# Last mixture of a decoder kernel: sorted rows that carry residual, weight and token; masks made by GpSimd

## The reference, cut to what matters

```
h = x + _attention(_rmsnorm(x, g1), wq, wk, wv, wo)
return h + _moe(_rmsnorm(h, g2), router_w, router_b, w1, w2, w3)

def _moe(x, router_w, router_b, w1, w2, w3):
    xf = x.reshape(n, d)                               # n = 2048
    vals, idx = jax.lax.top_k(xf @ router_w + router_b, 2)
    scores = jax.nn.softmax(vals, axis=-1)
    cap = int(np.floor(n * CAP_FRAC))                  # 256
    oh = jax.nn.one_hot(idx, E, dtype=jnp.float32)     # 8 experts
    pos = jnp.cumsum(jnp.cumsum(oh, axis=0), axis=1).astype(jnp.int32)
    emask = oh * (pos < cap)
    tmask = jnp.sum(emask, axis=-1)
    assign = jnp.einsum('tke,e->tk', emask, jnp.arange(E, dtype=jnp.float32)).astype(jnp.int32)
    m = jnp.max(assign, axis=-1)                       # one expert per token
    y = y_all[m, jnp.arange(n)]       # gelu((xf @ w2[m]) * (xf @ w1[m])) @ w3[m]
    slot = jnp.where(tmask[..., None] > 0, y[:, None, :], xf[:, None, :])
    return jnp.einsum('tkD,tk->tD', slot, scores)
```

## Time and profile before

| | us |
|---|---|
| median of 3 runs | 1674.38 |
| lowest, highest | 1672.79, 1678.52 |
| the profiled execution, its time | 1675.38 |
| its span, first to last instruction | 1673.6 |
| busy: PE, DVE, ACT, POOL | 1423.6, 966.6, 749.0, 232.3 |

### The profile page before, as it was taken

One profiled execution on the slowest core, in us unless ns is written; L12 is line 12 of the kernel. 1 busy time (PEld: TensorE's weight loads), 2 busy tenths in 40 slices (PEclk: granted clock), 3 DMA queues, 4 the chain that ended last, 5 costly groups with the idle time before them and its releaser, 6 DMA issues.

```text
span 1673.6 us, 43831 instructions
## 1 busy us (share of the span) xinstructions
PE 1423.6 (85%) x17681; PEld 878.2 (52%) x17681; DVE 966.6 (58%) x2541; ACT 749.0 (45%) x1927; POOL 232.3 (14%) x201
## 2 busy tenths in 40 slices
PE   4889888696499999999958999889989898999672
PEld 3343434393266666766633466346644564456462
DVE  4354635323477777777723676576665776477532
ACT  1323142251266666666613276327723672447431
POOL 1011120123030030200010200030002100120124
PEclk7989999797799999999978899999989998899897
DMA  9600000023230100100021000000000000000012
GB/s 327 264 17 1 17 1 7 17 58 98 77 140 4 26 19 10 35 4 16 4 76 43 1 2 2 5 7 2 2 5 7 2 2 1 7 1 1 6 55 70
DMA packets 62072, 60.07 MB, mean 36 GB/s; under 512 B 27952, under 2 KB 47024, under 8 KB 60720
## 3 DMA queue, kind: packets, MB, share of 16 engines
q1 hardware_dynamic: 59536, 53.04, 10.0%
q0 software_dynamic: 2048, 4.20, 0.9%
q10 hardware_dynamic: 288, 0.03, 0.0%
HBM read 32.73 MB, written 24.51 MB: 34 GB/s over the span
## 4 chain that ended last, share of the span: by engine, by line
PE 69%; DVE 15%; issue 4%; SPq 4%; DMA 3%; ACT 3%; POOL 2%; ACTq 0%; POOLq 0%; DVEq 0%
PE ps L1126 7%; PE ps L1514 6%; PE ps L1533 5%; PE ps L500 5%; PE ps L1547 4%; PE ps L1106 4%; PE ps L1116 4%; DVE arena L586 4%; PE ps L1147 4%; PE ps L258 4%; PE ps L1502 3%; PE ps L474 3%; PE ps L1161 2%; PE ps L1556 2%; PE ps L797 2%
## 5 line engine op out<-in xcount | busy, mean ns | idle before, releaser
L1259 DVE TENSOR_REDUCE nmax<-ps 128x1 f32<-128x512 f32 x256 | 166.8, 683 | 56.3 <-PE ps L1116 55.7
L1590 ACT ACTIVATE arena<-ps,arena 128x512 f32<-128x512 f32 (+3 forms) x256 | 135.5, 531 | 119.1 <-DVE arena L1650 112.9
L1650 DVE TENSOR_REDUCE arena<-ps 128x1 f32<-128x512 f32 (+3 forms) x256 | 124.3, 487 | 78.8 <-PE ps L1518 76.7
L1219 ACT ACTIVATE arena<-ps,nmax 128x512 f32<-128x512 f32 x172 | 119.0, 692 | 80.8 <-DVE nmax L1259 79.3
L1533 PE MATMUL ps<-sqc,arena 128*128 128x128 f32 x640 | 106.6, 287 | 20.0 <-DVE arena L1658 19.7
L586 DVE TENSOR_REDUCE arena<-ps 128x8 f32<-128x1232 f32 x64 | 89.2, 1438 | 40.3 <-PE ps L462 40.1
L258 PE MATMUL ps<-identb 128*128 128x512 bf16 x408 | 110.0, 430 | 1.4 <-DVE kcol L707 1.4
L1267 DVE COPY arena<-ps 128x512 f32<-128x512 f32 x128 | 88.0, 688 | 39.9 <-PE ps L1126 38.4
L1514 PE MATMUL ps<-arena 64*128 64x384 f32 (+3 forms) x512 | 106.2, 493 | 0.0
L1658 DVE TENSOR_SCALAR arena<-arena 128x512 f32<-128x512 f32 (+3 forms) x256 | 100.8, 394 | 9.1
L598 DVE RECIPROCAL arena<-ps 128x128 f32<-128x128 f32 x8 | 7.7, 959 | 160.4 <-PE ps L500 160.4
(11 more groups left out here) (350 smaller groups left out, 2713.1 us busy)
## 6 DMA issues: line engine op xcount, KB each, us to landing
xs_d<-onehot SPq DMA_DIRECT2D x3, 3072.0 KB, 29.6
cw<-in_cw SPq DMA_DIRECT2D x2, 2048.0 KB, 13.4
rv<-in_rv SPq DMA_DIRECT2D x2, 1536.0 KB, 19.7
late<-in_gw SPq DMA_DIRECT2D x3, 1024.0 KB, 10.8
arena<-xs_d SPq DMA_DIRECT2D x46, 64.0 KB, 1.8
xs_d<-arena SPq DMA_DIRECT2D x46, 64.0 KB, 1.6
xs_d<-onehot SPq DMA_DIRECT2D x1, 2560.0 KB, 22.4
onehot<-q_s SPq DMA_DIRECT2D x96, 8.0 KB
```

The lines of the kernel that those rows point to most:

```text
L1219: nc.scalar.activation(PB[k % 6], ps[:, k % 5, :], ACT.Exp, bias=nmax[:, u:u + 1], accum_out=rsum[:, b % 2, u:u + 1]).then_inc(SD["exp"], 1)
L1259: nc.vector.tensor_reduce(nmax[:, k % NU:k % NU + 1], ps[:, k % 5, :], AX.X, ALU.max, negate=True)\
L1590: nc.scalar.activation(TF["p%d" % (n % 2)][:, h * S:h * S + wd], ps[:, FSB[n % 2][h], 0:wd], ACT.Exp, bias=TF["nmax"][:, k4:k4 + 1], accum ...
L1650: nc.vector.tensor_reduce(TF["nmax"][:, k4:k4 + 1], ps[:, FSB[n % 2][h], 0:wd], AX.X, ALU.max, negate=True)\
```

## The change

**Rows of G.** The sorted rows become 258 floats wide (`GW4`): normed row, residual, kept weight, and a token number. They live in `G4`, which takes the place of `cw1` and `cw2` (now one tensor `cw`), and go to a new HBM buffer `gs_d` of 23,552 rows. The token number is stored less 4096, so that a row that was never sent, all zero, gives number 4096 after the correction, beyond the output's 2048 rows, and is dropped by the bounds check. DVE's last operation of a tile does weight * y + residual, and POOL scatters the tile straight to the output. The gathers, the adds, the write-back and the output stores go.

**Who does what.** The weight copies of G move from POOL to ACT, behind each `linear` and ahead of the gelu. POOL instead makes an index and issues one indirect DMA per tile. SP only loads. `gs_d` is zeroed by `pool_G_zero`, four DMAs from the POOL queue between `pool_C` and `pool_D`.

**Masks.** `dve_prepare` keeps only pcol and moves to `dve_X` ahead of `dve_masks`; the rest is `pool_prepare`, ahead of `selw` on POOL, with a semaphore `s_mask` for which DVE (before L410) and PE wait.

```diff
-            else:
-                dve_prepare(dve)
...
+            if b == 0:
+                dve.wait_ge(s_mask, 1)
...
             if k == "B" and b == 0:
+                dve_prepare(dve)
                 dve_masks(dve)
...
-            pe.wait_ge(s_prep, 4)
+            pe.wait_ge(s_mask, 1)
...
+        def pool_prepare(pool):
+
+            pool.wait_ge(s_const[1], 16 * len(GROUPS[1]))
+            nc.gpsimd.tensor_copy(xmask[:, :, 0:KP], xmask_in)
+            nc.gpsimd.tensor_copy(xmask[:, :, KP:KW], xmask_in[:, :, 0:KW - KP])
+            for mask, given in ((amask, amask_in), (kmask, kmask_in)):
+                nc.gpsimd.memset(mask[:, :, KS:KP], MASKED)
+                nc.gpsimd.tensor_scalar(mask[:, :, 0:KS], given[:, :, :], MASKED, None, ALU.mult)
+                ins = nc.gpsimd.tensor_scalar(mask[:, :, KP:KW], given[:, :, 0:KW - KP], MASKED, None, ALU.mult)
+            ins.then_inc(s_mask, 1)
+            nc.gpsimd.tensor_copy(cpick[:, :, :], causal_in[:, 0:2, :])
+            nc.gpsimd.tensor_copy(cmask[:, :, :], causal_in[:, 2:4, :]).then_inc(s_mask, 1)
+
         def dve_prepare(dve):
 
             dve.wait_ge(s_const[1], 16 * len(GROUPS[1]))
-            nc.vector.tensor_copy(xmask[:, :, 0:KP], xmask_in)
-            nc.vector.tensor_copy(xmask[:, :, KP:KW], xmask_in[:, :, 0:KW - KP])
-            for mask, given in ((amask, amask_in), (kmask, kmask_in)):
-                nc.vector.memset(mask[:, :, KS:KP], MASKED)
-                nc.vector.tensor_scalar(mask[:, :, 0:KS], given[:, :, :], MASKED, None, ALU.mult)
-                ins = nc.vector.tensor_scalar(mask[:, :, KP:KW], given[:, :, 0:KW - KP], MASKED, None, ALU.mult)
-            ins.then_inc(s_prep, 1)
-            nc.vector.tensor_copy(cpick[:, :, :], causal_in[:, 0:2, :])
-            nc.vector.tensor_copy(cmask[:, :, :], causal_in[:, 2:4, :])
             nc.vector.tensor_reduce(pcol[:, :], vmask[:, :, :], AX.X, ALU.max).then_inc(s_prep, 1)
-            dve.wait_ge(s_prep, 5)
+            dve.wait_ge(s_prep, 4)
...
+        GW4 = 2 * P + 2
+        G4 = cw[:, 0:NTT * GW4].rearrange("p (t n) -> p t n", n=GW4)
+        XBG = [cut(GW4) for _ in range(NXB)]
+        g_p = sb("g_p", [P, 1])
+        gidx = sb("g_idx", [P, 4], mybir.dt.int32)
+        gs_d = nc.dram_tensor("gs_d", (XROWS, GW4), F32, kind="Internal").ap()
+        out_rows = out.rearrange("b s d -> (b s) d")
...
-        yn4, xo4, yg4 = (lambda b, a=a: tiles_of(a, b) for a in (own4, x4, other4))
+        yn4, xo4 = (lambda b, k=k: G4[:, b * NT:(b + 1) * NT, k * P:(k + 1) * P] for k in range(2))
+        cy4 = lambda b: G4[:, b * NT:(b + 1) * NT, 2 * P]
...
         def pool_G_send(pool, b):
             pool.wait_ge(SG["slot"], b + 1)
-            for n in range(NT):
-                nc.gpsimd.indirect_dma_start(xs_d, bass.IndirectOffsetOnAxis(ap=slot4[:, b * NT + n:b * NT + n + 1], axis=0),
-                                             yn4(b)[:, n, :], None).then_inc(SC["sent"], 16)
+            if b == 0:
+                pool.wait_ge(SG["zero"], 16 * 4)
+            for n in range(b * NT, b * NT + NT):
+                nc.gpsimd.indirect_dma_start(gs_d, bass.IndirectOffsetOnAxis(ap=slot4[:, n:n + 1], axis=0),
+                                             G4[:, n, :], None).then_inc(SC["sent"], 16)
...
+            def weights(s):
+                e = act.value_load(expert4[0:1, s:s + 1], min_val=0, max_val=E2 - 1)
+                if s >= 2:
+                    act.wait_ge(SC["h"], NS + s - 1)
+                nc.scalar.copy(TG[f"w{s % 2}"].rearrange("p (m n) -> p m n", m=2),
+                               gw12[:, :, bass.ds(e, 1), :].rearrange("p m o n -> p m (o n)")).then_inc(SC["w1"], 1)
+
+            act.wait_ge(SG["table"], 1)
+            weights(0)
+            weights(1)
             linear(0)
...
+                if s + 2 < NS:
+                    weights(s + 2)
...
-                    dve.wait_ge(SC_st[s % 4], 16 * (st_c[s % 4] + s // 4))
-                V.tensor_copy(TG[f"y{s % 4}"], ps[:, 6 + s % 2, 0:P]).then_inc(SC["yb"], 1)
-            for b in range(B):
-                dve.wait_ge(SC_yg[b], 2 * 16 * NT)
-                for i in range(NT):
-                    ins = V.scalar_tensor_tensor(xo4(b)[:, i, :], yg4(b)[:, i, :], cy4[:, b * NT + i:b * NT + i + 1], xo4(b)[:, i, :],
-                                                 ALU.mult, ALU.add)
-                ins.then_inc(s_xout, 1)
+                    dve.wait_ge(SG_out[s % 4], 16 * (s // 4))
+                V.scalar_tensor_tensor(TG[f"y{s % 4}"], ps[:, 6 + s % 2, 0:P], XBG[s % NXB][:, 2 * P:2 * P + 1],
+                                       XBG[s % NXB][:, P:2 * P], ALU.mult, ALU.add).then_inc(SC["yb"], 1)
 
         def sp_G(sp):
             sp.wait_ge(SC["sent"], 2 * 16 * NTT)
             sp.wait_ge(SG["table"], 1)
-
-            def load(s):
+            for s in range(NS):
                 r = sp.value_load(rows4[0:1, s:s + 1], min_val=0, max_val=XROWS - P)
                 if s >= NXB:
-                    sp.wait_ge(SC["tx"], NS + s - NXB + 1)
-                sp.dma_start(XBG[s % NXB], xs_d[bass.ds(r, P), :]).then_inc(SC_ld[s % NXB], 16)
-
-            for s in range(NXB):
-                load(s)
+                    sp.wait_ge(SC["yb"], NS + s - NXB + 1)
+                    sp.wait_ge(SG["idx"], s - NXB + 1)
+                sp.dma_start(XBG[s % NXB], gs_d[bass.ds(r, P), :]).then_inc(SC_ld[s % NXB], 16)
+            for z in range(4):
+                sp.wait_ge(SG_out[z], 16 * st_c[z])
+
+        def pool_G_zero(pool):
+
+            zero = kmask[:, :, :].rearrange("p b n -> p (b n)").bitcast(F32)[:, 0:GW4]
+            nc.gpsimd.memset(zero, 0.0).then_inc(s_own, 1)
+            pool.wait_ge(s_own, 2)
+            rows = gs_d.rearrange("(p r) d -> p r d", p=P)
+            for z in range(4):
+                r0, r1 = z * XROWS // P // 4, (z + 1) * XROWS // P // 4
+                nc.gpsimd.dma_start(rows[:, r0:r1, :], zero.unsqueeze(1).to_broadcast([P, r1 - r0, GW4])).then_inc(SG["zero"], 16)
+
+        def pool_G(pool):
             for s in range(NS):
-                r = sp.value_load(rows4[0:1, s:s + 1], min_val=0, max_val=XROWS - P)
-                sp.wait_ge(SC["yb"], NS + s + 1)
-                sp.dma_start(xs_d[bass.ds(r, P), :], TG[f"y{s % 4}"]).then_inc(SC_st[s % 4], 16)
-                if s + NXB < NS:
-                    load(s + NXB)
-
-        def pool_G(pool):
-            pool.wait_ge(SG["table"], 1)
-            for s in range(NS):
-                e = nc.gpsimd.value_load(expert4[0:1, s:s + 1], min_val=0, max_val=E2 - 1)
-                if s >= 2:
-                    pool.wait_ge(SC["h"], NS + s - 1)
-                nc.gpsimd.tensor_copy(TG[f"w{s % 2}"].rearrange("p (m n) -> p m n", m=2),
-                                      gw12[:, :, bass.ds(e, 1), :].rearrange("p m o n -> p m (o n)")).then_inc(SC["w1"], 1)
-            for z in range(4):
-                pool.wait_ge(SC_st[z], 16 * 2 * st_c[z])
-            for n in range(NTT):
-                nc.gpsimd.indirect_dma_start(yg4(n // NT)[:, n % NT, :], None, xs_d,
-                                             bass.IndirectOffsetOnAxis(ap=slot4[:, n:n + 1], axis=0)).then_inc(SC_yg[n // NT], 16)
+                pool.wait_ge(SC_ld[s % NXB], 16 * (ld_c[s % NXB] + s // NXB + 1))
+                if s >= 4:
+                    pool.wait_ge(SG_out[s % 4], 16 * (s // 4))
+                nc.gpsimd.tensor_scalar(gidx[:, s % 4:s % 4 + 1], XBG[s % NXB][:, 2 * P + 1:GW4], 2.0 * B * S, None, ALU.add)\
+                    .then_inc(SG["idx"], 1)
+                pool.wait_ge(SG["idx"], s + 1)
+                pool.wait_ge(SC["yb"], NS + s + 1)
+                nc.gpsimd.indirect_dma_start(out_rows, bass.IndirectOffsetOnAxis(ap=gidx[:, s % 4:s % 4 + 1], axis=0),
+                                             TG[f"y{s % 4}"], None, bounds_check=B * S - 1, oob_is_err=False)\
+                    .then_inc(SG_out[s % 4], 16)
...
-            for b in range(B):
-                sp.wait_ge(s_xout, b + 1)
-                sp.dma_start(out[b:b + 1].rearrange("o (t p) d -> p (o t) d", p=P), xo4(b)).then_inc(s_store, 16)
-            sp.wait_ge(s_store, B * 16)
...
+            pe.wait_ge(s_mask, 2)
...
+            ch(nc.vector.tensor_reduce(g_p[:, 0:1], c["tri"], AX.X, ALU.add))
+            ch(nc.vector.tensor_scalar(g_p[:, 0:1], g_p[:, 0:1], -1.0, float(P - 2 * B * S), ALU.mult, ALU.add))
+            ch(nc.vector.tensor_scalar(G4[:, :, 2 * P + 1], row["index"][:, 0:NTT], float(P), g_p[:, 0:1], ALU.mult, ALU.add))
...
-            pool.wait_ge(s_const[1], 16 * len(GROUPS[1]))
+            pool_prepare(pool)
...
             pool_C(pool)
+            pool_G_zero(pool)
             pool_D(pool)
```

More of the change, by code:

```diff
@@ L133, in decoder @@
         cwg = sb("cwg", [P, E1])
-        cw1 = sb("cw1", [P, E1, HID1])
-        cw2 = sb("cw2", [P, E1 * HID1 // P, P])
+        cw = sb("cw", [P, 2 * E1 * HID1])
```

(17 more changed lines are left out.)

6 lines of the change are left out of this document (1 added, 5 removed).

## The result

The median is 1751.3 us (1745.7 to 1762.6, 4 runs) against 1676.5 us before (1672.8 to 1680.5, 4 runs): a ratio of 1.045, interval 1.039 to 1.052. The forecast was 1661 us, 1649 to 1676, faster. The kernel is slower by 75 us, and the prediction is wrong.

A forecast was written before the change was run, and what follows sets the result against it. Bound by a chain of waits: SP-paced tiles, then a last 28 us of POOL gathers and DVE's add. 1675.4 - 24.1 + 9.5 + 0.5 - 4.5 + 5 = 1661.8, given as a 1661 us median, range 1649 to 1676.

The forecast's parts named there:

- Zeroing gs_d: Four POOL DMAs from about 405 us, beside D0: +5 us, between 0 and +13.9, from contention with D0's transfers.
- Preparing the rows: POOL's zeroing DMAs: 2.9 ns per row, 17 us per DMA, 68 in all, hidden in D0 and D's first quarter.
- The rate: Zeroing's 24.3 MB would move at the 406 to 416 GB/s of the kernel's other zeroing, filling the DMA engines for 60 us.
- The share: D0's five DMA waits, 13.9 us: two queues sharing alike could double them; +5 if only the last three see load.
- The zeroing crowds D0 out: Rival, D0: small reads wait behind large pieces, the 13.9 could treble; +20 instead of +5, 1676 us; chance 0.10.
- POOL is late for D: Rival, spread(1) in D: four DMAs at 7.5 ns per row take 177 us, PE waits +53.5; 1710 us; chance 0.15.
- Tail: After the last tile's result: gathers, add and output stores go, 27.9 us removed, 3.8 in their place; net -24.1 us.
- Tile loop: G's 23 tiles: ACT's weight copy closes a cycle of 2.5 us per tile; +9.5 us (+5.5 to +11.5).
- the loop isn't bound by ACT: Rival, G's tile loop: expert number read while linear runs; 2.2 us per tile, 1653 to 1655 us; chance 0.12.
- Longer rows: G's last four sends and first load: rows grow from 512 to 1032 bytes; +0.5 us.
- Start: Kernel start: masks move to POOL, freeing DVE, PE's L346 ends 5.3 us earlier, some 0.8 given back; -4.5 (-2.5 to -5.3).

The follow-up runs named there:

- the two pairs: Changed kernel, zeroing in F, number read ahead of linear; masks on POOL against VectorE: 1648.5 and 1648.4 us; with rows of 272 floats: 1646.1 and 1651.6 us.

## Why the prediction was wrong

**Zeroing gs_d: this step failed.** The forecast had +5 for it; the same zeroing put alone into the kernel before cost 97 us of D0. Each of its sub-steps was off, and all in one direction; the failing one is the overlap, that D0 would pay for at most 13.9 us of it.
- *Preparing the rows.* I took 17 us per DMA, from how fast a 128-row send shows up among the transfers, so that two of D0's five waits would be over before the engines filled. A DMA of 5,888 rows holds POOL for 2.2 us, and the engines are full from 402 on. A bound made from an indirect send of 128 rows said nothing of a plain one of 5,888.
- *The rate.* I took the other zeroing's 406 GB/s, 60 us. It has 2,048-byte pieces, this one 1,032: 216 GB/s, 113 us. The text said for the sends that no row shows 1,032-byte pieces, but carried no doubt of it into this term.
- *The share.* I let equal turns double 13.9 us of waits. They became 101.2. The two queues moved 4,482 and 6,015 packets in D0 (q1 mean 1.05 KB, q0 4.06 KB), and by their shares a packet of q1 held an engine 0.08 us and one of q0 0.30. If they take turns by packet, one of D0's takes 4.8 times its own time, not twice; by this estimate 13.9 us become 66, and what makes them 101 no run separates. The Trainium skill ("DMA: Bandwidth & Descriptors", Queues, rings and completion order) gives turns by packet; the counts fit it but don't test it. My reading of it as "double" was wrong, since I compared times of transfers and not packets. Better had been the length of the zeroing itself as the upper end: a stage made of dependent small transfers, started beside a full queue, can lose all of it.

The upper end +13.9 was thus no bound, and the range ended at 1676. The rival *The zeroing crowds D0 out* had the right place and sign, at +20 and a chance of 0.10. The rival *POOL is late for D*, to which I gave more, didn't come: 0.4 ns per row, not 5.2; POOL stood 65 us in front of its third DMA, but its operands came 55 us before PE took them.

**Tail** (forecast -24.1): last result's start to the end 28.2 to 6.4, -21.8. The 3.8 us that I put in its place are 6.1: the last scatter can't start until the index operation has run, which itself stands behind the scatter before it (1754.12, 1755.23, 1756.24), 1.5 us that I had left out, and the span ends 3.5 us behind it, where my two rows (0.30 of issue and 2.24 to land) gave 2.5.

**Tile loop** (+9.5): +8.6. 2.51 us per tile, forecast 2.5, bound by ScalarE's number and copy; reading the number ahead of `linear` took 7.9 back. The rival that the loop isn't bound by ACT fell.

**Longer rows** (+0.5): +0.7 to the first result.

**Start** (-4.5): L327 -6.75, the last gather -5.6 and 6 to 8 in the two pairs. That is more than the 5.3 that I allowed, and what I had left out is the clock. L346's eight products took 1.49 us (0.73 and 0.76) against 2.42, and L355's 1.25 against this row of before:

```profile
29.76 2.29 PE L355 MATMUL ps<-arena 128*128 128x144 f32 x8
```

PE had stood idle 5.58 us ahead of L346 before, and 0.57 now; the mean granted clock behind it was 0.54 (23.5 to 37.3 us), near the lower of its two levels, and is 0.93 (20.0 to 30.5). The masks came at 26.0, wanted at 27.2. The Trainium skill ("GPSIMD Engine Reference", 2.1 Instruction dispatch) gives about 6 us for the first call to a freshly loaded library; the library's rows on POOL's queue stand at 19.2 and 19.3, and L717 starts at 19.38, so this trace doesn't agree, unless the library was not a fresh one. POOL's own pace was slower than I had it, 2.9 to 3.4 ns per element (1.79 us for 616), and it still fitted.

**The rest**: 8.9 us of the profiled execution's difference lie between D's first product and G's last send, with the granted clock at 0.94 against 0.95. The same stretch took 1134 to 1148 us in the four kernels with the zeroing in F, which differ in nothing there but the length of the rows, so I put it down to the clock. PE's busy time for the same 15,256 products bears that out, 1051.8 us against 1041.1; no run shows why the clock differed. The executions' median is 11 us below the profiled one.

Without the zeroing's term my sum would have been 1675.4 - 24.1 + 9.5 + 0.5 - 4.5 = 1656.8; the same with the measured -21.8, +8.6, +0.7 and -5.6 is 1657.3. That these two are 0.5 apart is luck: the four terms were off by +2.3, -0.9, +0.2 and -1.1. The version with the zeroing in F, 7.9 us better in the tile loop, measured 1648.5, where this sum gives 1657.3 - 7.9 - 1.0 = 1648.4, closer than executions that lie between 1637.5 and 1654.2 can tell.

## What to carry to other kernels

A large background transfer isn't free because nobody waits for it: ask which stages beside it are chains of small dependent transfers, and charge them up to its whole length (in the seven kernels with zeroing beside D0, D0 lost 0.69 to 0.85 of the time for which it kept the engines busy). A stage without a data transfer on its path isn't safe either, if an engine runs many small instructions there (D lost 48 us); F, with some 8 or 9 products per microsecond, lost nothing that shows. Take a transfer's rate only from one with the same piece length, and round rows in memory up to a multiple of 64 bytes. An engine's move of a copy into a loop is priced by the cycle that it closes; reading a loop's index ahead of the wait takes it out of the cycle.
